# The last product of an expert layer, by columns: which half of the tokens VectorE sums and which half TensorE folds

## What is computed

```python
logits = xt @ Wr + br                       # 8 experts
top_p, top_idx = jax.lax.top_k(softmax(logits), 2)
weights = top_p / top_p.sum(axis=-1, keepdims=True)
xn = layernorm(xt); xe = xn * ln_g[e] + ln_b[e]
h = gelu(xe @ W1[e] + b1[e])                # 64 -> 256
y = h @ W2[e] + b2[e]                       # 256 -> 64
out = xt + sum over the chosen e of weights[e] * y[e]
```

## Time and profile before

| what | value |
|---|---|
| time, median of 3 runs | 65.83 us (65.71 to 65.84) |
| the profiled execution's own time | 65.81 us |
| its span, from the first to the last instruction | 64.0 us |
| TensorE busy | 57.9 us (90%) |
| VectorE / ScalarE / GpSimd busy | 32.4 / 33.3 / 24.6 us |
| granted TensorE clock | 1.0 of full speed in every slice |

### The profile page before, as it was taken

One profiled execution on the slowest core, in us unless ns is written; L12 is line 12 of the kernel. 1 busy time (PEld: TensorE's weight loads), 2 busy tenths in 40 slices (PEclk: granted clock), 3 DMA queues, 4 the chain that ended last, 5 costly groups with the idle time before them and its releaser, 6 DMA issues.

```text
span 64.0 us, 1191 instructions
## 1 busy us (share of the span) xinstructions
PE 57.9 (90%) x356; PEld 33.2 (52%) x356; DVE 32.4 (51%) x152; ACT 33.3 (52%) x78; POOL 24.6 (38%) x48
## 2 busy tenths in 40 slices
PE   1987799799799999999999999999999999999940
PEld 0314356398445677955266285283643718722630
DVE  2367779458997799674007992040402204024730
ACT  5301337823349997709937729539195592930000
POOL 5165690000660895515059916143060003403500
PEclk9999999999999999999999999999999999999999
DMA  0442469720000000000056720006681000011011
GB/s 0 97 96 43 160 112 400 243 88 0 5 0 0 5 10 0 0 0 9 1 157 200 209 105 0 10 9 177 200 219 51 0 0 0 0 41 48 3 41 41
DMA packets 4270, 4.45 MB, mean 70 GB/s; under 512 B 2196, under 2 KB 2840, under 8 KB 4264
## 3 DMA queue, kind: packets, MB, share of 16 engines
q1 hardware_dynamic: 3944, 4.34, 22.9%
q10 hardware_dynamic: 320, 0.03, 0.5%
HBM read 4.08 MB, written 0.29 MB: 68 GB/s over the span
## 4 chain that ended last, share of the span: by engine, by line
PE 67%; DVE 18%; DMA 4%; SPq 3%; issue 3%; ACT 2%
PE banks L856 25%; PE banks L883 23%; PE banks L813 5%; DMA X<-in_x_dram 4%; DVE nmax L509 3%; PE banks L866 3%; PE banks L798 3%; DVE KS L503 2%; DVE X L495 2%; PE banks L835 2%; SPq L245 2%; PE banks L900 2%; ACT PR L378 2%; DVE T L527 2%; DVE X L559 1%
## 5 line engine op out<-in xcount | busy, mean ns | idle before, releaser
L414 ACT ACTIVATE H<-banks,PF 128x512 f32<-128x512 f32 x32 | 19.8, 683 | 9.3 <-PE banks L856 9.3
L856 PE MATMUL banks<-XE,W1F 64*128 64x256 f32 x128 | 16.8, 394 | 0.0
L883 PE MATMUL banks<-H,W2F 128*64 128x512 f32 x64 | 15.3, 603 | 0.0
L856 PEld LDWEIGHTS banks<-XE,W1F 64*128 64x128 f32 x128 | 11.4, 186 | 5.7 <-issue 4.4
L321 POOL TENSOR_TENSOR acc<-acc,gated 128x512 f32<-128x512 f32 (+1 forms) x6 | 6.5, 1088 | 16.5 <-DVE gated L639 16.5
L639 DVE SCALAR_TENSOR_TENSOR gated<-banks,B2T,GS 128x512 f32<-128x512 f32 (+1 forms) x7 | 4.6, 672 | 11.3 <-PE banks L883 11.3
L307 POOL TENSOR_SCALAR XE<-XF,PF,LB 128x256 f32<-128x256 f32 x15 | 8.2, 562 | 5.3 <-ACT XF L395 5.3
L754 PE MATMUL banks<-zeros 128*128 128x512 f16 x23 | 7.6, 450 | 1.3 <-POOL zeros L324 1.3
L291 POOL TENSOR_TENSOR rs<-base,half 128x4 f32<-128x4 f32 x4 | 4.0, 1012 | 9.9 <-DVE base L552 9.9
L883 PEld LDWEIGHTS banks<-H,W2F 128*64 128x64 f32 x64 | 4.0, 136 | 6.9 <-issue 6.7
L813 PEld LDWEIGHTS banks<-V,PTS 128*128 128x128 f32 x32 | 3.9, 191 | 0.9 <-issue 0.9
(11 more groups left out here) (78 smaller groups left out, 64.8 us busy)
## 6 DMA issues: line engine op xcount, KB each, us to landing
GS<-gates_kept SPq DMA_DIRECT2D x16, 128.0 KB, 3.0
W1F<-in_w_dram SPq DMA_DIRECT2D x1, 768.0 KB, 4.5
W2F<-in_w_dram SPq DMA_DIRECT2D x1, 512.0 KB, 5.0
W1F<-in_w_dram SPq DMA_DIRECT2D x1, 256.0 KB, 3.3
out_dram<-res SPq DMA_DIRECT2D x4, 64.0 KB, 1.6
X<-in_x_dram SPq DMA_DIRECT2D x2, 64.0 KB, 2.0
X<-in_x_dram SPq DMA_DIRECT2D x1, 128.0 KB, 2.5
WQK<-in_attn_w_dram ACTq DMA_DIRECT2D x2, 16.0 KB, 2.1
```

The lines of the kernel that those rows point to most:

```text
L414: nc.scalar.activation(H[:, r, :].rearrange("p (t n) -> p t n", t=PT), ps_z[g // J % 2][:, :, PIX * j:PIX * j + PIX], ACT.Gelu, bias=PF[:, ...
L856: nc.tensor.matmul(ps_z[q % 2][:, k, PIX * j:PIX * j + PIX], W1F[rows, e, j, :], XE[h][rows, e, :], start=True, stop=True).then_inc(z_read ...
L883: mm = nc.tensor.matmul(ps_y[s % 2][C * k:C * k + C, :], W2F[:, u, :], H[:, (2 * J * s + J * k + j) % RING, :], start=(j == 0), stop=(j == ...
```

## The change

The last step's layer 2 is computed in two parts by columns: first the even tiles for both experts and both parts of the contraction, into columns 0 to 255 of its usual bank, then the odd tiles into a bank of their own (bank 5, which the gates had used; hence the new wait on `gateT_ready`). The roles of the two halves of the columns in the fold are exchanged. VectorE's `weigh(7)` now covers the even columns alone; `add_last` adds the even product and the even part of `acc[1]`; and the odd product is made by a new function, `weigh_odd`, that stands behind `add_last` on VectorE. On TensorE `fold_even` folds the one sum, and `fold_odd` folds the odd part of `acc[1]` and then the odd product. The number of instructions on TensorE's fold, on VectorE and on GpSimd stays the same; layer 2 of the last step has sixteen records of 256 columns in place of eight of 512.

```diff
+        ps_y_odd = banks[:, 5, PIX:TOK]
...
-                cuts = 2 if s == STEPS - 1 else 1
-                for k in range(cuts):
-                    cols = slice(TOK // cuts * k, TOK // cuts * (k + 1))
-                    nc.vector.scalar_tensor_tensor(out=dst[:, cols], in0=ps_y[s % 2][:, cols], scalar=B2T[:, p:p + 1],
-                                                   in1=GS[s][:, cols], op0=ALU.add, op1=ALU.mult)\
-                        .then_inc(gated_ready, 1)
+                cols = slice(0, PIX) if s == STEPS - 1 else slice(0, TOK)
+                nc.vector.scalar_tensor_tensor(out=dst[:, cols], in0=ps_y[s % 2][:, cols], scalar=B2T[:, p:p + 1],
+                                               in1=GS[s][:, cols], op0=ALU.add, op1=ALU.mult).then_inc(gated_ready, 1)
+
+            def weigh_odd():
+
+                dve.wait_ge(y_ps, 2 * (STEPS + 1))
+                nc.vector.scalar_tensor_tensor(out=gated[1][:, PIX:TOK], in0=ps_y_odd, scalar=B2T[:, PAIRS - 1:PAIRS],
+                                               in1=GS[STEPS - 1][:, PIX:TOK], op0=ALU.add, op1=ALU.mult)\
+                    .then_inc(gated_ready, 1)
 
             def add_last():
 
-                dve.wait_ge(gated_ready, STEPS + 1)
-                dve.wait_ge(acc_ready, 2 * PAIRS - 2)
-                nc.vector.tensor_tensor(last_sum[:, :], gated[1][:, PIX:TOK], acc[1][:, PIX:TOK], ALU.add)\
+                dve.wait_ge(gated_ready, STEPS)
+                dve.wait_ge(acc_ready, 2 * PAIRS - 3)
+                nc.vector.tensor_tensor(last_sum[:, :], gated[1][:, 0:PIX], acc[1][:, 0:PIX], ALU.add)\
                     .then_inc(last_ready, 1)
...
             add_last()
+            weigh_odd()
             finish(1)
...
+                parts = [(slice(0, TOK), ps_y[s % 2])]
+                if s == STEPS - 1:
+                    pe.wait_ge(gateT_ready, HALVES)
+                    parts = [(slice(0, PIX), ps_y[s % 2][:, 0:PIX]), (slice(PIX, TOK), ps_y_odd)]
+                for cols, y in parts:
+                    for j in range(J):
+                        for k in range(2):
+                            u = J * (2 * p + k) + j
+                            mm = nc.tensor.matmul(y[C * k:C * k + C, :], W2F[:, u, :],
+                                                  H[:, (2 * J * s + J * k + j) % RING, cols],
+                                                  start=(j == 0), stop=(j == J - 1))
...
             def fold_even():
-
-                pe.wait_ge(acc_ready, 2 * PAIRS - 3)
+                pe.wait_ge(last_ready, 1)
                 pe.wait_ge(res_ready, IMG)
                 for k in range(IMG):
-                    nc.tensor.matmul(ps_end[0][:, k, :], acc[1][:, P * k:P * k + P], fold[:, :],
-                                     start=(k == 0), stop=False, skip_group_check=True)
-                pe.wait_ge(gated_ready, STEPS)
-                for k in range(IMG):
-                    last = nc.tensor.matmul(ps_end[0][:, k, :], gated[1][:, P * k:P * k + P], fold[:, :],
-                                            start=False, stop=True, skip_group_check=True)
+                    last = nc.tensor.matmul(ps_end[0][:, k, :], last_sum[:, P * k:P * k + P], fold[:, :],
+                                            start=True, stop=True)
                 last.then_inc(out_ps, 1)
 
             def fold_odd():
-                pe.wait_ge(last_ready, 1)
+
+                pe.wait_ge(acc_ready, 2 * PAIRS - 2)
                 pe.wait_ge(h_ready, HALVES * UNITS)
                 for k in range(IMG):
-                    last = nc.tensor.matmul(ps_end[1][:, k, :], last_sum[:, P * k:P * k + P], fold[:, :],
-                                            start=True, stop=True)
+                    nc.tensor.matmul(ps_end[1][:, k, :], acc[1][:, PIX + P * k:PIX + P * k + P], fold[:, :],
+                                     start=(k == 0), stop=False, skip_group_check=True)
+                pe.wait_ge(gated_ready, STEPS + 1)
+                for k in range(IMG):
+                    last = nc.tensor.matmul(ps_end[1][:, k, :], gated[1][:, PIX + P * k:PIX + P * k + P], fold[:, :],
+                                            start=False, stop=True, skip_group_check=True)
                 last.then_inc(out_ps, 1)
```

More of the change, by code:

```diff
@@ L879, in layer2 @@
                 pe.wait_ge(h_ready, 2 * J * (s + 1))
[L880 to L887, removed]
+                parts = [(slice(0, TOK), ps_y[s % 2])]
[9 more added lines that the diff above has]
+                                                  start=(j == 0), stop=(j == J - 1))
+                            if j == J - 1:
+                                mm.then_inc(y_ps, 1)
             def turn_b2():
```

## The result

| kernel | time, median | against the kernel before, 95% interval | span of the profiled execution | its time less its span |
|---|---|---|---|---|
| before | 65.81 us | | 64.02 | 1.80 |
| changed | 66.23 us | 1.0069 (1.0053 to 1.0084) | 64.36 | 1.89 |

The changed kernel is 0.42 us slower by the medians and 0.44 by the two profiled executions (65.81 and 66.25). Of the 0.44, the span has 0.35, which is what the prediction summed up; the other 0.09 lies outside the span and was in no term of the sum.

What follows compares the result with a forecast made beforehand. The end chain bounds it: the last `finish`, at 61.65 before, starts at 60.37 + 0.05 + 1.54 plus 0.04, 62.00, 0.35 later. So 65.81 becomes 66.16, given as 66.18 for the median; 8-in-10 range 65.75 to 66.40.

Steps and rivals of the forecast that it cites:

- The held add: VectorE's add into `last_sum`, moved forward, is held by GpSimd's odd cut: 0.85 to 0.9 us, not 0.42; chance 0.68.
- as if started 0.14 before GpSimd's end: Rule for the held add's end, from 32-column operations: 60.09 - 0.14 + 0.42 = 60.37.
- The rival in which the whole 0.42 comes after GpSimd's end: On VectorE, the add runs wholly behind GpSimd's odd cut, ending at 60.51; time 66.32, chance 0.10.
- its five cases: VectorE operations with two SBUF tensors begun under a GpSimd operation (lines 580, 602, 617), each ending 0.03 to 0.05 after it.
- whenever it began: Claim that a held VectorE operation ends 0.03 to 0.05 after GpSimd's operation, regardless of its own start.
- The split: Layer 2 by columns: even product ends at 59.20, under GpSimd's even cut ending 59.41, so costed at nothing.
- The fold: On TensorE, all twelve records follow the add from 60.42 and take 1.54, without pauses between groups.
- The rival "the add gets in first": VectorE's add slips in between GpSimd's two cuts, or is not held: 65.72, not slower; chance 0.18.
- the operation at 23.83: VectorE operation cited against the add getting in first: it came 0.15 after GpSimd's start and was held throughout.
- its deciding point: The delay after GpSimd's start from which VectorE's add is held, put somewhere under 0.15.
- The rival's time without the hold: With the add not held, the last `finish` starts at 61.54 against 61.65; time 65.72.

Runs made afterwards that it cites:

- four kernels with a held add: The changed kernel (66.23 us) and it with GpSimd's odd cut twice as long (66.78), behind a 128-column memset (66.38), or the fold of the odd sum first (66.05).
- the memset run: Changed kernel with GpSimd's odd cut replaced by a memset of another tile, which reads nothing: 65.83 us, 1.0000 to the kernel before.
- the PSUM run: Changed kernel with the even product in a free PSUM bank, so the add has one input in PSUM: 65.85 us, 1.0008 to the kernel before.
- The later cuts: Changed kernel with GpSimd's odd cut pushed back behind a memset of another tile: 128 columns 66.38 us, 256 columns 65.92 us.

## Why the prediction was right

- **The held add.** Forecast: start 59.46 to 59.52, end 60.37. Measured: 59.50 and 60.36. The distance of 0.28 behind GpSimd's end, carried over from operations of 32 columns by "as if started 0.14 before GpSimd's end", came out as 0.281 or 0.282 in all four kernels with a held add, under GpSimd operations of 0.72 and 1.26. The rival in which the whole 0.42 comes after GpSimd's end was wrong: the long add, like the short ones, ends 0.14 sooner than that. The prediction takes its five cases for all that there are; they aren't. The kernel before has five more operations with two SBUF tensors that begin under a GpSimd operation, in its last 0.04 to 0.06 us, and take their usual 0.17 to 0.18 (the second of line 602 twice, of line 617 once, line 590 twice). They agree with "as if started 0.14 before GpSimd's end", but not with "whenever it began".
- **The Trainium skill's rule**, "SBUF — State Buffer", section "Who interferes with whom". That a VectorE instruction with two SBUF inputs contends with a GpSimd instruction that reads SBUF, and not with one that only writes, agrees with the memset run (0.43 against 0.86). That one with at most one SBUF input does not contend, which the section says only for operations outside VectorE's 2-port perf modes, agrees with the PSUM run for the add (0.42). Lines 610 and 597 were held with one SBUF tensor; which mode they ran in no trace tells. That whoever issues first gets the shared ports does not hold by recorded starts: the add that started 0.003 ahead was held. There the measurement decides.
- **The split** was costed at nothing under GpSimd's cut: even product at 59.18 (59.20 forecast). In the span that is right. Outside the span it costs 0.09, and this step failed: the sum took what lies around the span as fixed at 1.80. For the profiled execution 66.16 was forecast and 66.25 came; the whole difference is this term.
- **The fold.** Start 60.41 (60.42), twelve records in 1.55 (1.54), no pause between the groups, last `finish` at 62.00 (62.00).
- **The rival "the add gets in first"** got 0.18 on the thought that the decision lies somewhere under 0.15 after GpSimd's start. The later cuts show that it lies before GpSimd's start, at a lead between 0.003 and 0.108 for VectorE. The add came 0.145 after it, as late as the operation at 23.83 that was held: that rival was priced too high, and its deciding point was on the wrong side. Line 602 in the kernel before had already hinted at that side. The rival's time without the hold was about right for the span: the last `finish` at 61.58 in the memset run, 61.54 forecast.

## What to carry to other kernels

Before an add with two SBUF tensors is moved on VectorE, look at what GpSimd does at its new place: a wait for the first of GpSimd's two cuts is worth little when the second cut starts at once and holds the add to its end. An input in PSUM avoided it here, and so did putting into that stretch a product with one tensor in PSUM and one in SBUF (0.48, not held). One SBUF tensor by itself is no safeguard: a tensor_scalar and a cast of that kind were held in the kernel before. And when an engine takes over a sum that another made in its idle time, count what now stands behind the last wait, not the instructions, whose number here was the same.

## What the runs showed of the hardware that was not expected

- GpSimd's add won against a VectorE add that started 0.003 us earlier; with 0.108 of lead VectorE won, and GpSimd's 256-column cut then took 0.90 in place of 0.72.
- Two VectorE operations with a single SBUF tensor, a tensor_scalar of 4 columns and a cast of 8, were held beside a GpSimd operation: 0.47 and 0.42 in place of 0.15 to 0.17 and 0.21.
- Eight more matmuls in the program, at the same length of the span, added 0.09 us outside it; a further eight added nothing.
